# Expert weights cut into 128-column tensors, second expert products as three fp16 terms, normed rows of the later rounds on ScalarE

## The reference

```python
h = jax.nn.gelu(xf @ w1e + b1e, approximate=False)   # tokens x hidden
y = h @ w2e + b2e                                    # tokens x 128
acc = acc + ce[:, None] * y
```

## Time and profile before

| | us |
|---|---|
| median of 3 runs | 1030.8 (1027.59 to 1034.84) |
| time of the profiled execution | 1034.46 |
| its span, first to last instruction | 1033.1 |
| TensorE matmul busy / weight load busy | 903.7 / 786.1 |
| VectorE / ScalarE / GpSimd busy | 563.8 / 476.0 / 493.5 |
| mean granted TensorE clock | 0.952 |

### The profile page before, as it was taken

One profiled execution on the slowest core, in us unless ns is written; L12 is line 12 of the kernel. 1 busy time (PEld: TensorE's weight loads), 2 busy tenths in 40 slices (PEclk: granted clock), 3 DMA queues, 4 the chain that ended last, 5 costly groups with the idle time before them and its releaser, 6 DMA issues.

```text
span 1033.1 us, 25972 instructions
## 1 busy us (share of the span) xinstructions
PE 903.7 (87%) x8524; PEld 786.1 (76%) x8524; DVE 563.8 (55%) x2208; ACT 476.0 (46%) x804; POOL 493.5 (48%) x519
## 2 busy tenths in 40 slices
PE   4478999998999599999899999996999999999860
PEld 2237999986899577899898898983778878778850
DVE  6785800055787065785038500588793988874022
ACT  3224454348654358645345444452538354454320
POOL 0551047073015771007474561776744447477765
PEclk9768999999999899999999999998999999999995
DMA  9946764452352543363452356832633143436772
GB/s 317 385 148 175 214 142 104 96 116 47 63 113 81 121 83 76 54 173 101 114 121 65 90 125 137 164 83 66 112 103 100 53 100 88 100 97 157 159 162 74
DMA packets 219623, 126.02 MB, mean 122 GB/s; under 512 B 137456, under 2 KB 199792, under 8 KB 219248
## 3 DMA queue, kind: packets, MB, share of 16 engines
q1 hardware_dynamic: 203120, 90.77, 37.2%
q0 software_dynamic: 16384, 33.59, 11.8%
HBM read 40.13 MB, written 56.90 MB: 94 GB/s over the span
## 4 chain that ended last, share of the span: by engine, by line
PE 57%; DVE 16%; POOL 9%; DMA 7%; issue 7%; ACT 4%; SPq 0%; POOLq 0%; ACTq 0%; DVEq 0%
PE bank L1530 21%; PE bank L1506 6%; PE bank L1508 5%; PE bank L1507 5%; POOL rows L2214 5%; POOL got L2234 4%; PE bank L1392 3%; DMA got<-y_l,slot_index 3%; PE bank L1345 2%; DMA turned<-rows 2%; PE bank L1528 2%; PE bank L1321 2%; PE bank L1364 2%; DVE x_res L2030 2%; PE bank L1402 2%
## 5 line engine op out<-in xcount | busy, mean ns | idle before, releaser
L1530 PE MATMUL bank<-blocks_l,hid 128*128 x2496 | 361.5, 287 | 0.0
L2214 POOL DMA_INDIRECT rows<-rows_sent,slot_index x192 | 186.3, 970 | 325.5 <-issue 248.3
L2234 POOL DMA_INDIRECT got<-y_l,slot_index x256 | 243.8, 953 | 188.9 <-PE bank L1530 74.5
L1530 PEld LDWEIGHTS bank<-blocks_l,hid 128*128 128x128 f32 x2496 | 312.1, 192 | 6.3 <-issue 1.3
L1678 ACT ACTIVATE hid<-bank 128x512 f32<-128x512 f32 (+1 forms) x316 | 185.2, 592 | 262.0 <-PE bank L1508 255.4
L1506 PE MATMUL bank<-turned,blocks_l 128*128 128x128 f16 x1248 | 238.9, 224 | 41.5 <-DMA turned<-rows 25.6
L2030 DVE SCALAR_TENSOR_TENSOR x_res<-got,share,x_res 128x128 f32<-128x128 f32 x256 | 78.2, 348 | 321.8 <-DMA got<-y_l,slot_index 319.4
L1508 PE MATMUL bank<-turned,blocks_l 128*128 128x128 f16 x1248 | 238.8, 224 | 0.0
L1507 PE MATMUL bank<-turned,blocks_l 128*128 128x128 f16 x1248 | 237.5, 223 | 0.0
L1506 PEld LDWEIGHTS bank<-turned,blocks_l 128*128 x1248 | 125.7, 101 | 56.2 <-issue 51.5
L1507 PEld LDWEIGHTS bank<-turned,blocks_l 128*128 x1248 | 124.6, 100 | 4.1 <-issue 1.3
(11 more groups left out here) (209 smaller groups left out, 1230.0 us busy)
## 6 DMA issues: line engine op xcount, KB each, us to landing
y_l<-y SPq DMA_DIRECT2D x92, 256.0 KB
blocks_l<-in_w_dram SPq DMA_DIRECT2D x4, 1536.0 KB, 17.1
got<-in_w_dram SPq DMA_DIRECT2D x16, 256.0 KB, 6.5
got<-y_l,slot_index POOLq DMA_INDIRECT x256
rows<-own SPq DMA_DIRECT2D x1, 3584.0 KB, 14.5
rows<-own SPq DMA_DIRECT2D x7, 512.0 KB, 4.1
hid<-in_w_dram SPq DMA_DIRECT2D x12, 256.0 KB, 5.3
rows<-rows_sent,slot_index POOLq DMA_INDIRECT x192, 2.7
```

The lines of the kernel that those rows point to most:

```text
L1530: m = t.do.matmul(out, hid[:, j * H + c * P:j * H + c * P + P], second[:, at], start=False, stop=(c == C - 1))
L2214: d = g.do.indirect_dma_start(rows_dram[s], at, rows[:, 2 * D * i:2 * D * i + 2 * D], None)
L2234: d = g.do.indirect_dma_start(got_mem[slot][:, col:col + D], None, y_dram[layer][s][layer.team(ev.i)], at)
```

## The change

Each layer's weights become one tensor for each 128-column piece: `firsts` (high and low) and `seconds` (high and low), each holding that piece of every expert side by side, and a small `select` tensor. The register holds the expert's number, and a piece's offset is the same multiple of it in every tensor. The second weights are now loaded raw in 28 parts of 256 KB like the first ones, and split: ScalarE rounds them times 32 to the high part (`upper_w2`), TensorE makes the rest by two products (`second_left`), ScalarE copies it as the low part (`lower_w2`). Gelu writes back into the PSUM bank; ScalarE copies it times 16 as fp16 to the high part of `hid`, VectorE makes the low part (`low_hidden`); the bank is held until then. The second product is three fp16 products for each piece: high by high, high by low, low by high. The scales come out in the copy of the outputs. The normed tiles of rounds 1 to 3 are made by ScalarE (`place_norm`) from a factor and an offset that VectorE leaves. Parking takes 8 DMAs each way. The planner's costs, banks and the table `EARLIER` are new.

```diff
+W2_PARTS = [[Ev(f"w2_{n}", 0, 0, u) for u in range(layer.chunks * layer.parts if layer.terms else layer.chunks)] ...]
-BANKS = {... "l1": (1, SC), ...
+BANKS = {... "l1": (1, None), ... "halve_0": (1, SC), "halve_1": (1, SC), ...
 # class Plan, the planner
         def second(ev):
+            yield Take(raw, [ev], 1)
             yield from self.stage(*ev)
+            yield from self.stage("upper" + ev.kind[2:], 0, 0, ev.i)
+            yield from self.stage("halve" + ev.kind[2:], 0, 0, ev.i, {PE: lambda: self.give(raw, ev)})
         def second(unit):
             yield Await(["halved"])
+            if layer.terms:
+                yield Take(self.hid, [l1], 1)
+                yield from self.stage("hid", s, p, unit, {VE: lambda: self.give(self.banks, (l1, 0))})
             yield Await([("l1", s, p, min(unit + FIRSTS_AHEAD, units[-1]))])
 ...
-EARLIER = {...}
+EARLIER = {...}     # other numbers
 ...
+        firsts = {layer: [cuts(layer, "first_high"), cuts(layer, "first_low")] for layer in LAYERS}
+        seconds = {layer: [cuts(layer, "second_high"), cuts(layer, "second_low")] ...}
+        select = {layer: sb(f"select_{layer.name}", [P, layer.E], F16) for layer in LAYERS}
 # TensorE
+            def second_left(ev, layer):
+                ...
+                t.do.matmul(bk[:, :], ccol("ident"), raw, start=True, stop=False)
+                t.wait_ge(*w2_high.after(Ev("upper" + ev.kind[5:], *ev[1:])))
+                m = t.do.matmul(bk[:, :], minus, part_of(seconds[layer][0], layer, ev), start=False, stop=True)
+            def cut_of(mem, e):
+                return mem[:, :].rearrange("p (e h) -> p e h", h=P)[:, bass.ds(e, 1), :].rearrange("p e h -> p (e h)")
             def layer1(ev):
-                        t.do.matmul(out, high[:, at], xh, start=True, stop=False)
-                        t.do.matmul(out, high[:, at], xl, start=False, stop=False)
-                        m = t.do.matmul(out, low[:, at], xh, start=False, stop=True)
+                        t.do.matmul(out, cut_of(high[c], e), xh, start=True, stop=False)
+                        t.do.matmul(out, cut_of(high[c], e), xl, start=False, stop=False)
+                        m = t.do.matmul(out, cut_of(low[c], e), xh, start=False, stop=True)
             def layer2(ev):
+                    t.wait_ge(*hidden_high[ev.s].after(Ev("hid", *ev[1:])))
+                    t.do.matmul(out, spread(select[layer][:, bass.ds(e, 1)]), bcol(...), start=True, stop=False)
-                    for c, at in enumerate(spans(C)):
-                        m = t.do.matmul(out, hid[:, ...], second[:, at], start=False, stop=(c == C - 1))
+                    for c in range(C):
+                        t.do.matmul(out, upper, cut_of(high[c], e), start=False, stop=False)
+                        t.do.matmul(out, upper, cut_of(low[c], e), start=False, stop=False)
+                    t.wait_ge(*hidden_low[ev.s].after(Ev("hid", *ev[1:])))
+                    for c in range(C):
+                        m = t.do.matmul(out, lower, cut_of(high[c], e), start=False, stop=(c == C - 1))
 # ScalarE
+            def place_norm(ev):
+                a.wait_ge(*norm_done[ev.s].after(ev))
+                ...
+                for i in range(BT):
+                    m = a.do.activation(xn[:, D * i:D * i + D], x[:, BT * ev.i + i, :], ACT.Identity, bias=minus_mean, scale=root)
+            def upper_w2(ev, layer):
+                a.do.activation(part_of(seconds[layer][0], layer, ev), raw, ACT.Copy, scale=W_SCALE).then_inc(w2_high.sem, 1)
+            def lower_w2(ev, layer):
+                a.do.activation(part_of(seconds[layer][1], layer, ev), bank_of(ev)[:, :], ACT.Copy, scale=W_SCALE).then_inc(w2_low.sem, 1)
+            def hid_free(l1):
+                if old: a.wait_ge(*expert_out[old.s].after(Ev("l2", *old[1:])))
+                else:
+                    a.wait_ge(*w1_low.after_all(w1_splits[0]))
+                    second_ready(a, L0)           # all low parts of the second weights
+            def hidden(ev):
+                a.do.activation(out, hb, ACT.Gelu, scale=1 / (X_SCALE * W_SCALE))      # out is the bank
+            def high_hidden(ev):
+                a.wait_ge(*hidden_gelu[ev.s].after(l1))
+                hid_free(l1)
+                m = a.do.activation(hid[:, 0:n], bank_of(l1)[:, 0:n], ACT.Copy, scale=HID_SCALE)
 # VectorE
+            def low_hidden(ev):
+                v.wait_ge(*hidden_high[ev.s].after(ev))
+                m = v.do.scalar_tensor_tensor(hid[:, SEQ:SEQ + n], bank_of(l1)[:, 0:n], HID_SCALE, hid[:, 0:n], ALU.mult, ALU.subtract)
             def norm(ev):
+                if ev.p:
+                    m = v.do.scalar_tensor_tensor(minus_mean, mean, -1.0, rstd, ALU.mult, ALU.mult)
+                    return
 # SyncE
+            def park_blocks(ev):
+                second_ready(y, L1)
+                for dram, mem in zip(pieces_dram, pieces[L1]):
+                    y.do.dma_start(dram, mem[:, :]).then_inc(block_parked.sem, 16)
```

More of the change, by code:

```diff
@@ L57, in __init__ @@
         self.groups = self.tiles // BT
-        self.block = 2 * hidden + 4
+        self.parts = experts // PART_EXPERTS
     def team(self, b):
@@ L193 @@
 SCORE_TILES = [(0, 1, 3 * P), (2, 1, 0), (1, 2, 0), (3, 0, 0)]
-W1_PARTS = [[Ev(f"w1_{n}", 0, 0, u) for u in range(layer.E // layer.unit)] for n, layer in enumerate((L0, L1))]
-SECOND_LOADS = 4
-W2_PARTS = [[Ev(f"w2_{n}", 0, 0, i) for i in range(SECOND_LOADS)] for n in range(2)]
+W1_PARTS = [[Ev(f"w1_{n}", 0, 0, u) for u in range(layer.chunks * layer.parts)] for n, layer in enumerate((L0, L1))]
+W2_AFTER = 5
+W2_PARTS = [[Ev(f"w2_{n}", 0, 0, u) for u in range(layer.chunks * layer.parts if layer.terms else layer.chunks)] for n, layer in enumerate((L0, L1))]
 def last_in_bank(at):
@@ L578, in normed @@
             yield Await([lead])
-        yield from self.stage(*norm)
-        self.mark(norm)
+        yield from self.stage(*norm, {VE: lambda: self.mark(norm)})
         if norm_end(lead) == norm:
@@ L798, in made @@
                     self.give(self.turned, Ev("fetch", s, p, unit // per_group))
-            yield Take(self.hid, [Ev("l1", s, p, unit)], 1)
-            yield from self.stage("l1", s, p, unit, {PE: made})
+            if not layer.terms:
+                yield Take(self.hid, [Ev("l1", s, p, unit)], 1)
+            yield from self.stage("l1", s, p, unit, {PE: made} if layer.terms else {PE: made, SC: lambda: self.give(self.banks, (Ev("l1", s, p, unit), 0))})
             self.spawn(second(unit), rank)
@@ L957, in macaron_program, with cuts @@
         bias = sb("bias", [P, BIAS_KEPT], F16)
[L958 removed]
+        def cuts(layer, name, dt=F16):
+            return [sb(f"{name}_{layer.name}_{c}", [P, layer.E * P], dt) for c in range(layer.chunks)]
+        firsts = {layer: [cuts(layer, "first_high"), cuts(layer, "first_low")] for layer in LAYERS}
+        seconds = {layer: [cuts(layer, "second_high"), cuts(layer, "second_low")] if layer.terms else [cuts(layer, "second", F32)] for layer in LAYERS}
+        select = {layer: sb(f"select_{layer.name}", [P, layer.E], F16) for layer in LAYERS}
+        pieces = {layer: [mem for half in firsts[layer] + seconds[layer] for mem in half] for layer in LAYERS}
         slot_index = [sb(f"slot_index{s}", [P, TOP_K, NT], I32) for s in range(STREAMS)]
@@ L965, in macaron_program, with buffers @@
         xn_mem, xt_mem = slots("xn", 2), slots("xt", 2)
-        parked = blocks[L1][:, 0:len(PARKED_SETS) * EARLY_BUFFERS * SEQ].rearrange("p (i n c) -> p i n c", n=EARLY_BUFFERS, c=SEQ)
+        def buffers(mem):
+            words = mem[:, :] if mem.dtype == F32 else mem[:, :].bitcast(F32)
+            return [words[:, at:at + SEQ] for at in range(0, words.shape[1], SEQ)]
+        parked = [buffer for mem in pieces[L1] for buffer in buffers(mem)]
+        late = [buffer for mem in pieces[L0][:-2] for buffer in buffers(mem)]
@@ L980, in macaron_program @@
+        assert len(late) >= 6 * LATE_SETS + 2 * LATE_ROWS
+        late_weights, late_const = (mem[:, :].bitcast(F32)[:, 0:n] for mem, n in zip(pieces[L0][-2:], (WCOLS - WEIGHTS_KEPT, CCOLS - CONST_KEPT)))
         rows_all = sb("rows_sent", [P, ROW_BUFFERS, SEQ], F32)
@@ L1054, in set_of @@
             i = pool.at[user]
-            return [mem[i][:, n, :] for n in range(mem[i].shape[1])], small[i]
+            return mem[i], small[i]
         def xn_of(role, ev):
@@ L1246, in bank_read, with normed, xn_read @@
             return attn_exp[s].after(ev, last_in_bank(j))
+        def normed(norm):
+            return (norm_placed if norm.p else norm_done)[norm.s].after(norm)
+        def xn_read(old):
+            if old.kind == "l2":
+                return [expert_out[old.s].after(old)]
+            turn = Ev("turn_" + old.kind[-1], *old[1:])
+            reads = [turned[old.s].after(turn)]
+            return reads + [rows_high[old.s].after(turn), rows_low[old.s].after(turn)] if turn.kind == "turn_g" else reads
         def x_written(ev):
```

(8 more changed lines are left out.)

271 lines of the change are left out of this document (169 added, 102 removed).

## The result

The changed kernel takes 1157.5 us (median of 4 runs, 1157.19 to 1157.74), the kernel before in the same comparison 1031.9 (4 runs, 1027.59 to 1034.84): ratio 1.121, 95% interval [1.117, 1.126]. The forecast was 1015 in a range of 980 to 1075; the result lies on the other side and beyond the range. The profiled execution took 1157.4, span 1156.1, granted clock 0.940.

A forecast was written before the change was run, and what follows sets the result against it. TensorE was taken to bound most of the span, its array barely covering the sequencer's addresses; stretch gains, less start +7 and banks and waits +4, summed to -16: 1018 for the profiled run, so 1015, range 980 to 1075.

The forecast's parts named there:

- failed step: TensorE's sequencer in expert units: a single address addition costs 85 ns, between bounds of 46 and 125.
- break-even of 95: Units of L0: nothing is gained once a single address addition costs 95 ns.
- the sequencer is the new bound: TensorE's queue in expert units: additions over 95 ns make the kernel slower, 1083 us at 110 ns; chance 0.19.
- Array: TensorE's products in expert units: 83 us less in all, 1.40 us a unit of L0, 1.46 of L1.
- ScalarE and VectorE: Copies, low parts and moved norms: ScalarE 476 to 744 us, VectorE 564 to 732, hidden where experts stand alone.
- Banks and waits: PSUM banks of first products held some 3.2 us instead of 1.5, plus extra waits: 4 us charged.
- The start: Before the first second product: splitting second weights adds 7 us, between bounds of 0 and 27.
- The gain given back: Stretches not TensorE's alone, start and banks get longer: +9 us, 1040 in all; chance 0.24.
- rival 2: Stretches with attention, the start and bank holds lengthen and cancel the gain: 1040 us; chance 0.24.
- its term for 198 to 502: Two phases of experts beside the other stream's attention: none of the 8 us gain arrives, ScalarE being over 130 of 147.
- Signs named in advance: Profile after: L0 unit spacing, separate addition records, longer gap at stream change, VectorE's chain share rising in 703 to 930.
- rival 1: Sequencer's address work sets expert units: L0 units 1.9 us apart, 1083 us at 110 ns an addition; chance 0.19.

The follow-up runs named there:

- Fixed experts: Changed kernel with each tile's expert a constant in the program, so TensorE's sequencer makes no addresses and loads no registers (values wrong): 1040.9 us, ratio 1.009.
- addresses ahead: Complete changed kernel with each tile's addresses made before its products, up to six additions to one instruction: 1039.7 us, ratio 1.010 to the kernel before.
- short low parts: Changed kernel, addresses packed before the products, VectorE making 32 of 512 columns of each hidden low part: 1195.0, 1196.4, 1214.4 us on slower chips (ratios 1.001, 1.004, 1.011).

## Why the prediction was wrong

**The failed step** is the price of a single address addition: taken as 85 ns, the middle between 46 and 125, with the reason that record and surroundings are "about that far from either end". Measured: 112 to 113. The break-even of 95 that the prediction gave lies between the two, so its sign followed from this number alone. The rows that spoke against 85 were in the argument itself: three operations in one instruction cost 125 and show as 46, so 79 lie outside the record. What is outside the record did not shrink with the operations: a single one shows as 32, and 79 + 32 = 111. At 85 the record would have had to be 6. The rival "the sequencer is the new bound" has this mechanism and was given 0.19.

**Its size** was short too: 1083 at 110 ns, 1157 measured at 112. The unit of L0: 1.90 was priced, 2.07 measured (median of 120). 94 of them have nothing on the sequencer but their 17 address instructions, which at their usual distances make 0.129 + 0.115 + 15 x 0.112 = 1.92. In 81 of the 94 exactly two of these distances are longer than usual, as at 602.24 above, together by 0.13 (median), which gives 2.05; what lengthens them no run shows. Units with a load of expert numbers lose another 0.5, for which the prediction had no term either. For L1 2.04 was priced and 2.21 measured (34 units). And of what a unit loses little was counted where attention stands beside it: +6 for the stretches up to 502, where 39 came, and +11 after 615, where 32 came. A part of both is the clock: TensorE is busy 79 us at the lower level instead of 47.

**Array**: right. Fixed experts and addresses ahead give 1.396 us a unit of L0, forecast 1.40, and 1.452 of L1, forecast 1.46.

**ScalarE and VectorE**: totals near (720 and 725, forecast 744 and 732), one term wrong. A normed tile on ScalarE was priced at 286 ns from an activation out of PSUM without factors. It takes 486, against 355 on VectorE:

```profile
L1693 ACT ACTIVATE xn<-x_res,norm 128x128 f32<-128x128 f32 x132 | 54.3, 486 | 46.8 <-DVE norm L1950 46.7
L1800 ACT ACTIVATE bank<-bank 128x512 f32<-128x512 f32 x308 | 179.0, 587 | 176.1 <-PE bank L1583 170.2 <-issue 4.3
L1807 ACT ACTIVATE hid<-bank 128x512 f16<-128x512 f32 x308 | 180.1, 598 | 14.3 <-PE bank L1619 10.1
```

78 us of work instead of 46. That the total came out below the forecast all the same is partly luck: busy time counts overlapping instructions once, and while it grew by 244 us, the durations summed grew by 291, where the forecast had 268. Moving the norms pays nonetheless, by 70 to 76 us under the new table and 25 under the old. The second row is gelu back into PSUM: 587 ns against the 598 of the earlier trace rows into SBUF. The Trainium skill, "ScalarE: Activation LUTs", section "Step-by-step: what each stage is for", says that writing to PSUM is faster; the trace agrees, by 11 ns, 3 us in 308.

**Banks and waits** were charged 4 us. TensorE waits for low parts 8 us in the changed kernel, 5.5 of them at first products that wait for a bank. It is 20 us with addresses ahead, where units are shorter.

**The start**: right in kind, short in size. Forecast +7 and the first second product at 102; the first product of the experts moves from 86.2 to 98.3 and the first second product from 94.70 to 105.0.

```profile
98.35 0.22 PE L1581 MATMUL bank<-turned,first_high_l 128*128 128x128 f16 x1
105.01 0.22 PE L1614 MATMUL bank<-second_high_l,hid 128*128 x1
```

**The gain given back** (rival 2, 0.24): it is true of the kernel with addresses ahead, with its places, the start and the rounds with causal attention; its term for 198 to 502, none of the gain, fits too (-15 and +14). That its 1040 meets the 1039.7 is partly luck: its size in the last rounds was short, the stretches of experts alone gave a larger gain than it had, and it had no term for the clock. That VectorE's load is the cause is supported by the norms' 25 to 76 us and by the waits, and not shown: the short low parts were to show it and didn't. Open as well is how much of 1040 an order made for units of 1.4 us would win, since two tables differ by 71 us.

**Signs named in advance**: units 1.9 apart pointed to rival 1, units of 1.67 or more against the forecast (2.07 came), and single additions stand as records of their own, all seen. The shares of the chain that ended last sum to only 61% in the profile after, so the 8% of VectorE (16% before) says neither yes nor no. Instead of a longer gap at the change of streams (12 us), 384 to 396 shows TensorE busy for 4.2 us.

## What to carry to other kernels

Count the register instructions in front of a stage's products and give each a full 110 to 140 ns, whatever is in it, and 650 to each load of a register; compare their sum with the array's time in the same stage, and if it comes near, ask for the addresses together ahead of the products. A cheaper product can make the sequencer the bound. And before a split into more terms, look at which engine makes the terms: in stretches where that engine serves the other stream's chain, its added work may cost more than its duration (25 to 76 us for 50 here), and where TensorE waits its granted clock was lower too.

## What the runs showed of the hardware

- Register instructions of TensorE's sequencer: a single addition shows as 32 ns and takes 112 to 113, the longer ones show as 51 and take 129, or as 74 (six operations) and take 133 to 138. Loading a register shows as 590 and takes 650.
- Such instructions are hidden as long as their sum stays below the array's time: 13 of them under 1.67 us, not 17 under 1.40.
- With addresses ahead TensorE's granted clock is 1.00 in the stretches where it is 98% busy and 0.88 in the one where it is 74% busy; at the lower level fp16 products of 128 columns start 0.107 us apart instead of 0.056.
- An activation of 128x128 from SBUF to SBUF with factor and offset for each partition takes 486 ns; VectorE's like operation 355.
- Chips differ: the kernel before takes 1031 us on two of them and 1192 and 1200 on two others, with unchanged durations of the instructions, a granted clock of 0.92 instead of 0.95, and releasers that the profile can't name.
